# Expert gate and up products in two 64-column tiles of TensorE, with the tokens of an expert staged by ScalarE

## What is computed

```python
scores = softmax(flat_x @ gate_w.T).T
topk_weight, topk_idx = jax.lax.top_k(scores, C)        # C = 74 tokens per expert
xg = flat_x[topk_idx]
g = jnp.einsum('ecd,eid->eci', xg, Wg)
u = jnp.einsum('ecd,eid->eci', xg, Wu)
h = jax.nn.gelu(g, approximate=False) * u
eo = jnp.einsum('eci,edi->ecd', h, Wd)
eo = eo * topk_weight[..., None]
flat_out = jnp.zeros_like(flat_x).at[topk_idx.reshape(-1)].add(eo.reshape(-1, d))
out = flat_out.reshape(b, s, d) + shared
```

## Time and profile before

| | |
|---|---|
| median of three runs | 821.31 us |
| the profiled execution's span | 819.1 us |
| TensorE busy with products (PE) / with weight loads (PEld) | 801.5 us / 751.4 us |
| VectorE / ScalarE / GpSimd busy | 633.9 / 460.6 / 251.6 us |
| weight loads and products of L1139 (gate and up) | 1024 of each, from 128.1 to 299.6 us |

### The profile page before, as it was taken

One profiled execution on the slowest core, in us unless ns is written; L12 is line 12 of the kernel. 1 busy time (PEld: TensorE's weight loads), 2 busy tenths in 40 slices (PEclk: granted clock), 3 DMA queues, 4 the chain that ended last, 5 costly groups with the idle time before them and its releaser, 6 DMA issues.

```text
span 819.1 us, 16629 instructions
## 1 busy us (share of the span) xinstructions
PE 801.5 (98%) x6060; PEld 751.4 (92%) x6060; DVE 633.9 (77%) x1287; ACT 460.6 (56%) x829; POOL 251.6 (31%) x297
## 2 busy tenths in 40 slices
PE   9999999999999999999999999999999999999988
PEld 8998789999999999899999989999998999999758
DVE  5786693778778876778797887878778787876796
ACT  4386424433333336585786777667687767745421
POOL 0002120410111100364366147335525623633020
PEclk9999999999999999999999999999999999999999
DMA  5010946998889812010210021031012103010001
GB/s 191 1 52 1 373 124 253 328 323 310 317 309 337 321 53 107 1 40 14 100 44 0 17 98 38 13 102 38 4 39 72 38 13 102 26 82 1 1 0 30
DMA packets 18290, 88.36 MB, mean 108 GB/s; under 512 B 3120, under 2 KB 7472, under 8 KB 12240
## 3 DMA queue, kind: packets, MB, share of 16 engines
q1 hardware_dynamic: 18256, 87.90, 30.4%
HBM read 85.05 MB, written 2.84 MB: 107 GB/s over the span
## 4 chain that ended last, share of the span: by engine, by line
PE 47%; issue 23%; POOL 18%; DVE 8%; ACT 3%; DMA 1%; POOLq 0%; SPq 0%; DVEq 0%; ACTq 0%
PE bank L1139 14%; POOL W_L L2000 7%; PE bank L1176 6%; POOL HF_L L2058 4%; POOL arena L1981 3%; POOL WQKV_L L2000 3%; PE bank L746 2%; PE bank L872 2%; PE bank L1185 2%; PE bank L722 2%; PE bank L1049 2%; PE bank L788 1%; POOL SQ L2019 1%; PE bank L1123 1%; PE bank L1490 1%
## 5 line engine op out<-in xcount | busy, mean ns | idle before, releaser
L1139 PE MATMUL bank<-arena 128*128 (+1 forms) x1024 | 117.8, 274 | 0.0
L1139 PEld LDWEIGHTS bank<-arena 128*128 128x128 f32 x1024 | 117.4, 192 | 0.0
L1981 POOL TENSOR_TENSOR arena<-arena,srec 111x456 f32<-111x456 f32 x56 | 52.3, 962 | 125.1 <-DVE srec L2153 125.1
L2000 POOL TENSOR_TENSOR W_L<-LW,W_H 128x256 fp32r<-128x256 f32 x96 | 68.5, 752 | 36.9 <-DVE XHL L2589 33.5
L2058 POOL TENSOR_TENSOR HF_L<-arena,HF_H 128x296 fp32r<-128x296 f32 x48 | 43.8, 937 | 76.7 <-ACT HF_H L1896 76.7
L788 PE MATMUL bank<-XHL,W_H 128*128 128x296 f32 x288 | 65.1, 307 | 0.0
L1896 ACT ACTIVATE arena<-bank,vec 128x296 f32<-128x296 f32 x96 | 48.8, 509 | 20.4 <-PE bank L788 15.4
L2012 POOL TENSOR_TENSOR QW<-QW,arena x14 | 22.4, 1600 | 119.0 <-DVE QW L2490 65.6
L1330 PE MATMUL bank<-HF_L,W_H 128*128 128x296 f32 x192 | 57.4, 299 | 0.0
L1330 PE MATMUL bank<-HF_H,W_H 128*128 128x296 f32 x192 | 57.4, 299 | 0.0
L1330 PE MATMUL bank<-HF_H,W_L 128*128 128x296 f32 x192 | 57.3, 299 | 0.0
(11 more groups left out here) (276 smaller groups left out, 2205.4 us busy)
## 6 DMA issues: line engine op xcount, KB each, us to landing
arena<-ew_in SPq DMA_DIRECT2D x16, 2048.0 KB, 9.0
arena<-ew_in SPq DMA_DIRECT2D x16, 1024.0 KB, 7.0
LW<-lw_in SPq DMA_DIRECT2D x12, 1024.0 KB, 5.0
arena<-route SPq DMA_DIRECT2D x32, 185.0 KB, 3.2
LW<-lw_in SPq DMA_DIRECT2D x6, 768.0 KB, 4.3
fp_weights<-arena SPq DMA_DIRECT2D x1, 2048.0 KB, 6.4
arena<-fp_weights SPq DMA_DIRECT2D x1, 2048.0 KB, 7.2
arena<-patches_in SPq DMA_DIRECT2D x2, 864.0 KB, 7.4
```

The costliest lines, as they stand in the source:

```text
L1139: last = mm(o[:, m * CAP:(m + 1) * CAP], w[:, kc, mi * P:(mi + 1) * P], xg(kc, e), start=(kc == 0), stop=(kc == C - 1))
L1981: nc.gpsimd.tensor_tensor(v, v, srec[0:QROWS, s:s + 2, :].unsqueeze(3).to_broadcast([QROWS, 2, C * JH, KEYS]), ALU.mult).then_inc(p_ready, 1)
L2000: last = nc.gpsimd.tensor_tensor(low[:, cols], value[:, cols], high[:, cols], ALU.subtract)
```

## The change

Each product of a 128-column weight becomes two products of 64 columns. The first writes PSUM partitions 0 to 63 and the second 64 to 127, so they are placed on the left and the right 64 columns of the array. The token operand is read from a new buffer `XGS[partition, slot, chunk, 74]` with two slots, whose address is fixed for each half of the loop, and not from `XG`. ScalarE fills it: both first slots amid the copies of `XG`, and then, after each `expert_out`, the slot of the expert after next. A semaphore `xg_staged` holds the gate product until the slot is filled. ScalarE's loop has six passes instead of seven, and its last pass is written out, because the last expert stages nothing.

```diff
@@ buffers
+COL_TILE = P // 2
+        XGS_AT = R_BASE + 4 * (2 * EM * D + EM * CAP)
+        XGS = nc.alloc_sbuf_tensor_at("XGS", [P, 2, C, CAP], F32, offset=XGS_AT)
@@ TensorE: expert_up
                 if u == 0:
                     pe.wait_ge(ld_gu[s], group(e) * 16 + 16)
-                xg = XGE[s]
+                    pe.wait_ge(xg_staged, plus(e, 1))
...
                     for m in range(4):
                         for kc in range(C):
-                            mi = 4 * half + m
-                            last = mm(o[:, m * CAP:(m + 1) * CAP], w[:, kc, mi * P:(mi + 1) * P],
-                                      xg(kc, e), start=(kc == 0), stop=(kc == C - 1))
+                            for lo in range(0, P, COL_TILE):
+                                at = (4 * half + m) * P + lo
+                                last = mm(o[lo:lo + COL_TILE, m * CAP:(m + 1) * CAP], w[:, kc, at:at + COL_TILE],
+                                          XGS[:, s, kc, :], start=(kc == 0), stop=(kc == C - 1))
@@ ScalarE: after the copy of xg4
+                if i == 4:
+                    act.wait_ge(moe_act, MOE_ACT["xg1"])
+                    for e in range(2):
+                        f(XGS[:, e, :, :], XG[:, :, e, :], ACT.Copy).then_inc(xg_staged, 1)
+            def stage_tokens(e, s):
+                f(XGS[:, s, :, :], XG[:, :, e, :], ACT.Copy).then_inc(xg_staged, 1)
@@ ScalarE: one expert in the loop
                 expert_out(e1 * 2, e1)
+                if staged:
+                    stage_tokens(i * 2 + (s + 1), 1 - s)
                 high_hidden(e1 * 2 + 2, i * 2 + s)
...
-            with act.Fori(1, E // 2) as i:
+            with act.Fori(1, E // 2 - 1) as i:
                 for s in range(2):
...
+                    expert_of(i, s)
+            expert_of(E // 2 - 1, 0)
+            expert_of(E // 2 - 1, 1, False)
```

More of the change, by code:

```diff
@@ L190, in build @@
         HH_H = over("HH_H", R_BASE, 2 * EM * D, [P, EM * CAP])
-        assert R_BASE + 4 * (2 * EM * D + EM * CAP) <= here()
+        XGS_AT = R_BASE + 4 * (2 * EM * D + EM * CAP)
+        XGS = nc.alloc_sbuf_tensor_at("XGS", [P, 2, C, CAP], F32, offset=XGS_AT)
+        assert XGS_AT + 4 * 2 * C * CAP <= here()
         const = sb("const", [P, CONST_W])
@@ L444, in build @@
         sw_full, eot_split = sem("sw_full"), sem("eot_split")
+        xg_staged = sem("xg_staged")
         ut_lead, ut_split = sem("ut_lead"), sem("ut_split")
@@ L1148, in idx @@
                 return e if isinstance(e, int) else e[0] * 2 + e[2]
-            def xg_ap(kc, e):
-                return XG[:, kc, idx(e), :]
-            XGE = [xg_ap, xg_ap]
             def plus(e, k):
@@ L1740, in _ @@
                        ACT.Copy), f"xg{i}")
+                if i == 4:
+                    act.wait_ge(moe_act, MOE_ACT["xg1"])
+                    for e in range(2):
+                        f(XGS[:, e, :, :], XG[:, :, e, :], ACT.Copy).then_inc(xg_staged, 1)
+            act.wait_ge(moe_act, MOE_ACT["xg7"])
+            def stage_tokens(e, s):
+                f(XGS[:, s, :, :], XG[:, :, e, :], ACT.Copy).then_inc(xg_staged, 1)
             def expert(e2, first):
@@ L1789, in _ @@
             expert_out(0, 0)
+            stage_tokens(2, 0)
             high_hidden(2, 1)
@@ L1792, in _, with expert_of @@
             high_weights("qkv", 0)
-            with act.Fori(1, E // 2) as i:
-                for s in range(2):
[L1795 to L1799, removed]
+            def expert_of(i, s, staged=True):
+                e1 = i * 2 + (s - 1)
+                expert(e1 * 2 + 2, False)
+                high_down(i * 2 + s, i, s)
+                expert_out(e1 * 2, e1)
+                if staged:
+                    stage_tokens(i * 2 + (s + 1), 1 - s)
+                high_hidden(e1 * 2 + 2, i * 2 + s)
+            with act.Fori(1, E // 2 - 1) as i:
+                for s in range(2):
+                    expert_of(i, s)
+            expert_of(E // 2 - 1, 0)
+            expert_of(E // 2 - 1, 1, False)
             expert_out(2 * (E - 1), E - 1)
```

## The result

The changed kernel takes 806.71 us (median of four runs, 805.27 to 808.71) and the kernel before 821.56 us beside it (820.75 to 822.17). The ratio is 0.9823, 95% interval 0.9805 to 0.9840: 15 us faster. I had forecast 830 us and slower. The time lies in the range, and almost on the 805 us of the rival in which the tiles work side by side.

What follows compares the result with a forecast made beforehand. The prediction took TensorE to bound the kernel, its gate and up blocks paced by weight loads. 32 blocks at +0.28 us add 9 us to the 821.3 us median, everything else nothing: 830 us, range 802 to 839.

Steps and rivals of the forecast that it cites:

- side by side: Gate and up blocks: both tiles load and multiply independently, block 2.00 us, end 799 to 811, middle 805 us; chance 0.26.
- The view of what bounds the kernel: Expert stretch: only TensorE in the chain; gate and up blocks paced by weight loads, 110 ns per load-product pair, streams hidden.
- The failing step: Gate and up blocks: second tile's load waits for first tile's second product; block 3.81 us, +9 us; chance 0.38.
- its cap from the DMA share: Expert stretch, in the side by side case: DMA busy 0.90 of 22.02 us, so two experts take at least 19.8 us.
- Entering and leaving the tiles: 64 changes between whole and half tiles cost nothing; 0.17 us each, 11 us in all, kept for the range's upper side.
- The price of half as many columns: Gate and up weight loads: a load of 64 columns takes 55 to 58 ns in place of 110.
- The staging at nothing: ScalarE's 16 copies of tokens, 0.2 to 0.42 us each, are hidden and cost nothing; 6 us in all if uncovered.
- TensorE never waits there: Expert stretch: TensorE runs without waits, so the +9 us of 32 longer blocks all goes into the end.
- only as far as VectorE and DMA allow: Gate and up blocks: shortening them helps only until VectorE (17.70 of 22.02 us) or DMA (0.90 of the time) limits.

Runs made afterwards that it cites:

- e1: The changed kernel with both 64-column halves of each gate and up product on the left column tile, one after the other; 848.41 us, ratio 1.0332.
- e10: e9 with an expert's two routing rows loaded in one transfer of longer packets in place of two; 800.07 us, ratio 0.9787.
- e4: The changed kernel loading only the gate half of the gate and up weights from the third expert on (output wrong); 806.01 us, ratio 0.9814.
- e9: The changed kernel with VectorE's sum over an expert's routing weights formed by the instruction that makes the products; 805.47 us, ratio 0.9787.
- e3: The changed kernel with each half block's products reordered: all of the left tile first, then all of the right; 829.93 us, ratio 1.0102.
- e2: The kernel before plus only ScalarE's staging copies and the waits on them, with whole products of 128 columns; 821.57 us, ratio 1.0002.
- e6: The changed kernel with `EOT_L` ahead of `EWD_L` on VectorE and the halved weight loads of e4 (output wrong); 809.83 us, ratio 0.9858.

## Why the prediction was wrong

**The view of what bounds the kernel held.** Blocks were paced by loads, and the streams were hidden under them. On a tile the pass of 64.4 ns (e1) lies near the 62.5 ns of a stream and above the 55 ns of a half load, so there the streams are the longer half, and with two tiles side by side 221 ns became 139.

**The failing step** is "A load does not start before the product ahead of it in the program ... I take it that this order holds for two tiles too", and the placing of the second tile's first load behind the first tile's second product. It starts beside the first tile's first load, as the three short windows show, and a block takes 2.22 us where the step made it 3.81. The row under that step was one block entry on whole products, which has only one tile to load. I carried it to a case that no row showed, against a rival that named this very point, and gave it 0.38 against 0.26. The Trainium skill (TensorEngine Tiling (Array Packing), Key Properties) says that tiles load and multiply independently; the trace agrees (e1 against the changed kernel, 4.26 and 2.22 us). The factor of up to 2 that this page gives for 64 columns (Theoretical Speedup) is not reached: 3.53 to 2.22 is 1.59.

That the time lies in the range is no merit of this step: the range reached down to 802 us only to take in the rivals.

**The rival "side by side"** was right in its mechanism and nearly in its number: 2.22 us for a block where it had 2.00 (139 ns for a product, not 125), two experts at 20.25 us where its cap from the DMA share was 19.8, and the end at 806.7 where it had 805. Its reason for the cap was half of the truth. The transfers do end near 19.3 us per two experts (e10), but VectorE, which it called "next", is a bound at the same place: in the changed kernel TensorE waits 15.5 us for `EOT_L` and 2.5 for weights, and neither fewer bytes (e4) nor less VectorE work (e9) alone moves the median by more than 1.2 us. So its 805 us is in part luck: it had no term for VectorE's waits, for the clock or for the changes of tile.

**Entering and leaving the tiles** I had costed at nothing by the earlier trace rows. The blocks behind tiles show otherwise: 0.16 us more for a down block and 0.14 for a scatter, 4.8 us in all (and the same in e1 and e3). Each of these blocks has a change on either side, so a change costs about 0.075 us, less than half of the 0.17 us of the earlier trace rows that I had kept for the range only. The Trainium skill (TensorEngine Tiling (Array Packing), Key Properties) says that a change of the tiling mode drains TensorE; the longer blocks fit that. Why show no such cost isn't settled. It is not the second tile in flight, since e1 has only one at work and pays the same. The 64-column products of the earlier trace rows are transposes (L1228, `nc.tensor.transpose`), and whether a transpose enters a tile at all no run shows.

**The price of half as many columns** (55 to 58 ns a load) can't be told from a block's length, since the streams of a tile last longer: a load and its product on a tile take 69 ns of it (2.22 us / 32, two tiles at once). At the entry of a block the second load of a tile begins 55 ns after its first, the lower end of the forecast.

**The staging at nothing** was right (e2, and no wait on `XGS`). **"TensorE never waits there"** held only for a longer block; for the shorter one the second half of the sentence in the first part, "only as far as VectorE and DMA allow", was what counted.

**Not in the prediction at all** was a fall of the clock: behind some of the waits that replace the work it fell, which cost 1.3 us in the changed kernel, 6.9 in e4 and 9.8 in e6.

## What to carry to other kernels

Where, as here, a float32 product loads 128 columns and streams 74 or 64, its loads pace it, and two column tiles that alternate in the queue take about 0.6 of the time in long rows and 0.73 in a row of three, less some 0.15 us for each block of whole products that stands between two blocks of tiles. Before counting that gain, look for the next two bounds in the same stretch (here 17.7 us of VectorE and 19.3 us of transfers under 22.0 of TensorE): easing one of two that lie so close gave at most 1.2 us here, in part because the lower clock took back what the shorter waits had given. A row that shows an order for one resource is no evidence for two; where a rival names the point on which all turns and no row shows it, the chances should be even.

## What the hardware showed that I had not expected

- Two column tiles on the same 128 rows load and stream at once: both first loads and products begin within 0.02 us. Products of one tile start up to three places ahead of queued ones of the other (e3), so only near neighbours in the queue run side by side: 3.68 us for a block with the tiles one after the other, 2.22 us alternating.
- On one tile the passes begin 64.4 ns apart (e1, without the block's first step), near the 62.5 ns that 74 columns take at the pace of the earlier trace rows. The block's mean, 66.6 ns (4.26 us for 64), also holds that first step and the change behind it.
- A stand of 1.5 us in TensorE was followed by a granted clock of 0.61 and a block of 3.52 us in place of 2.22 (e4), five times; the stands before the scatters of the changed kernel, up to 1.9 us, were followed by gate blocks of 2.22 to 2.29 us at a granted clock of 1.00, and only behind the last one did the clock fall (0.66 in the last down block). Part of the work taken off TensorE came back in this way.
- VectorE's step L2536 took 1.57 us in one expert and 0.83 in the next. GpSimd's part of the rounding (L2030) runs beside both: 0.94 us of the long one at 176.88 us, and 0.55 us of the short one at 185.73. Whether it makes the difference was not tested.
